# ScalarE's copy of the second group's transposes moved behind four exponentials in an attention kernel

## The chip, the core and the metric

The kernel runs on one NeuronCore of a Trainium2 chip. The metric is the device time of one execution in microseconds (us). The engines are TensorE (PE, with PEld for its weight loads), VectorE (DVE), ScalarE (ACT), GpSimd (POOL) and SyncE (SP), which only issues transfers here.

## What is computed

The input is 64 x 128 rows ("b h") of 128 positions by 64 channels, in float32. Each row is an attention of its own over its 128 positions, behind a batch norm with given mean and variance:

```python
xn = (x - moving_mean) * jax.lax.rsqrt(moving_var + BN_EPS) * gamma + beta
q = xn @ Wq + bq
k = xn @ Wk + bk
v = xn @ Wv + bv
scores = jnp.einsum('bhid,bhjd->bhij', q, k) * d ** (-0.5)
attn = jax.nn.softmax(scores, axis=-1)
out = jnp.einsum('bhij,bhjd->bhid', attn, v)
out = out @ Wo + bo
return xn + out
```

## The kernel before

The kernel folds norm and weights once at the start. w_g stands for the product of the query and key weights, w_o for that of the value and output weights. The 8192 rows are worked in 1024 groups of 8 rows, and the program goes through 512 steps of two groups each: in step t, an even group 2t and an odd group 2t+1 ("the second group"). Each engine has its own instruction stream, written out by hand in its function step(r, t, peeled); the loop body holds four steps, with a few peeled steps ahead of it and behind it. The order on an engine is the order of the calls in its step, and the engines wait for each other by semaphores. A group passes through these stages, several steps apart:

- GpSimd weighs x (L277), adds the bias (L288) and, for three groups of four, makes the last sum y (L299). For the fourth, every other step, VectorE scales in place and adds (L455, L466).
- TensorE projects xT with w_g into one half of tg_ps (L682, two projections a step). ScalarE copies each into g (L360, keep_g).
- TensorE makes the scores of a group in score_ps from g and xT (L624). VectorE finds the row maxima (L490 in two halves for the even group, L480 for the odd) and from them the shift neg_top (L501, L511).
- ScalarE makes the exponentials, 8 a group, one for each row, each with the read of its sum (L335, two instructions each in the profile). The first of an even group waits for neg_top_a_found, the fifth for neg_top_b_found.
- TensorE transposes the 8 probability matrices into tg_ps (L670). For an even group ScalarE copies one half into probsT (L349) and VectorE the other (L549). For an odd group ScalarE copies all of it (L351, keep_probsT).
- TensorE multiplies probabilities and x (L643), VectorE copies the result to uT (L521), TensorE applies w_o (L692), and VectorE scales by the inverted sums into attn (L446).

tg_ps is one buffer of two banks, used in turn by the transposes of the even group, the transposes of the odd group and the two projections. TensorE's projections of step t therefore wait for probsT_a_kept of group 2t-1, which the copy L351 of the same step signals, and the output pair that stands last in the step waits for it and for both copies of g. The odd scores wait for probs_found of the odd group of the step before, since they overwrite its scores.

Of the kernel before, what the change touches and what calls it, by code (L numbers as in the profile page):

```python
# [17 lines left out]
def build(nc: bass.Bass, x, gamma, beta, mean, var, wq, bq, wk, bk, wv, bv, wo, bo, out):  # L18
# [12 lines left out]
    with ExitStack() as ctx:  # L31
# [121 lines left out]
        def uses(r, n):  # L153
            return count(r, n, SEMS, 1)
# [13 lines left out]
        def parts(n):  # L168
            return n % SEMS
# [7 lines left out]
        def pipeline(eng, step):  # L177
            for t in range(-4, BODY):
                step(0, t, True)
            with eng.Fori(2, N // BODY - 1) as r:  # L180
                turn = Turn(eng, r)
                for t in range(BODY // 2):
                    step(turn, t, False)
            for t in range(BODY // 2 + 4):
                step(N // BODY - 1, t, True)
# [5 lines left out]
        def exists(r, n, peeled):  # L191
            return not peeled or 0 <= group(r, n) < N
# [119 lines left out]
        @block.scalar  # L312
        def _(act):
            for i, v in enumerate((gamma, beta, mean, var)):
                act.dma_start(norm_col[:, i:i + 1], v.rearrange("(c o) -> c o", o=1)).then_inc(params_loaded, DMA_INC)
                act.dma_start(norm_row[:, i, :], v.rearrange("(o c) -> o c", o=1).broadcast_to([128, C])).then_inc(params_loaded, DMA_INC)
            act.wait_ge(dve_setup, ROW_VAR)
            nc.scalar.activation(col_tmp[:, 1:2], col_tmp[:, 0:1], ACT.Sqrt).then_inc(act_setup, 1)
            nc.scalar.activation(row_tmp[:, 1, :], row_tmp[:, 0, :], ACT.Sqrt).then_inc(act_setup, 1)

            nc.scalar.activation(exp_first[:], norm_col[:, 3:4], ACT.Exp, scale=-1.0)

            def exponentials(r, n, peeled, rows):
                if not exists(r, n, peeled):
                    return
                s = parts(n)
                if 0 in rows:
                    act.wait_ge((neg_top_a_found if n % 2 == 0 else neg_top_found)[s], uses(r, n))
                    if exists(r, n - 4, peeled):
                        act.wait_ge(probsT_made[s], uses(r, n - 4))  # L330
                        act.wait_ge(sum_inverted[parts(n | 1)], uses(r, (n - 4) | 1))
                for q in rows:
                    if q == HALF and n % 2 == 0:
                        act.wait_ge(neg_top_b_found[s], uses(r, n))
                    last = nc.scalar.activation(probs[:, n % 4, q, :], score_ps[n % 2][:, q // PAIRS, q % PAIRS * W:(q % PAIRS + 1) * W],  # L335
                                                ACT.Exp, bias=neg_top[:, s, q:q + 1], accum_out=prob_sum[:, s, q:q + 1])
                    if q == GROUP - 1:
                        last.then_inc(probs_found[s], 1)

            def keep_probsT(r, n, peeled):  # L340

                if not exists(r, n, peeled):
                    return
                s = parts(n)
                act.wait_ge(probsT_made[s], uses(r, n))
                if exists(r, n - 4, peeled):
                    act.wait_ge(u_made[s], uses(r, n - 4))
                if n % 2 == 0:
                    nc.scalar.activation(probsT_parts[n % 4][:, :, 0], probsT_halves[:, :, 0], ACT.Copy).then_inc(probsT_a_kept[s], 1)  # L349
                else:  # L350
                    nc.scalar.activation(probsT_parts[n % 4], probsT_halves, ACT.Copy).then_inc(probsT_a_kept[s], 1)  # L351

            def keep_g(r, n, peeled):
                if not exists(r, n, peeled):
                    return
                s = parts(n)
                act.wait_ge(g_made[s], uses(r, n))
                if exists(r, n - 4, peeled):
                    act.wait_ge(scores_made[s], uses(r, n - 4))
                nc.scalar.activation(g[:, s].rearrange("p k w -> p (k w)"), tg_ps[:, n % 2],  # L360
                                     ACT.Identity, bias=g_bias[:, 0:1]).then_inc(g_kept[s], 1)

            def step(r, t, peeled):
                keep_probsT(r, 2 * t - 2, peeled)
                exponentials(r, 2 * t, peeled, range(0, 2))
                keep_probsT(r, 2 * t - 1, peeled)
                exponentials(r, 2 * t, peeled, range(2, 8))
                keep_g(r, 2 * t + 2, peeled)
                keep_g(r, 2 * t + 3, peeled)
                exponentials(r, 2 * t + 1, peeled, range(0, 8))  # L370

            pipeline(act, step)

        @block.vector
# [358 lines left out]
```

## Time and profile before

| | us |
|---|---|
| median of 3 runs | 4721.29 (4721.06 to 4724.11) |
| the profiled execution | 4727.12 |
| its span, first to last instruction | 4724.9 |
| PE busy | 4540.1 (96%) |
| DVE busy | 4495.3 (95%) |
| POOL busy | 4508.7 (95%) |
| ACT busy | 4297.6 (91%) |

The granted clock of TensorE is 0.998 of full speed over the span. Busy time is the time with an instruction on the engine; the page further names the chain of work that ended last, the costliest groups of instructions by line with the idle time ahead of them, and the releaser of that idle time. A timeline row gives the start in us from the start of the span, the duration, the engine, the line, the operation and its output and inputs, and in brackets the idle time ahead of it and the engine and line that ended it. Matmul ends are modelled. A row with x4 or x16 is a run of such instructions.

### The profile page before, as it was taken

The page shows a single profiled execution, that of the slowest core. Times are in us where ns is not written, and L with a number is a line of the kernel's source. Part 1 is how long each engine was busy: PE and PEld are TensorE (multiplying, and loading weights), DVE is VectorE, ACT ScalarE, POOL GpSimd, SP SyncE. Part 2 cuts the span into 40 slices and gives each one's busy share as a digit, 9 for nine tenths or more (in the row PEclk, how much of TensorE's full clock was granted, in tenths as well). Part 3 has the DMA queues.
Part 4 walks back from the last instruction along what each step waited for, and adds up shares of the span by engine and source line. Part 5 has one row for each costly group of instructions (what it writes and reads, how often), then busy time and mean ns, then how long its engine had stood idle before and what let it go on. Part 6 is the DMA issues. An engine that isn't in the chain of part 4 may idle for free.

```text
span 4724.9 us, 187136 instructions
## 1 busy us (share of the span) xinstructions
PE 4540.1 (96%) x59416; PEld 3778.9 (80%) x59416; DVE 4495.3 (95%) x7970; ACT 4297.6 (91%) x18437; POOL 4508.7 (95%) x2824
## 2 busy tenths in 40 slices
PE   7999999999999999999999999999999999999999
PEld 5888888888888888888888888888888888888887
DVE  7999999999999999999999999999999999999998
ACT  7999999999999999999999999999999999999998
POOL 7999999999999999999999999999999999999998
PEclk9999999999999999999999999999999999999999
DMA  7888888888888888888888888888888888888886
GB/s 141 174 173 172 173 172 172 172 173 172 173 171 172 172 172 172 172 173 173 171 173 173 172 173 171 172 172 172 172 172 172 173 171 172 173 172 173 171 173 139
DMA packets 4294236, 806.28 MB, mean 171 GB/s; under 512 B 4294208, under 2 KB 4294208, under 8 KB 4294208
## 3 DMA queue, kind: packets, MB, share of 16 engines
q1 hardware_dynamic: 4293312, 805.80, 85.3%
q8 instruction: 15, 0.25, 0.0%
q10 hardware_dynamic: 896, 0.13, 0.0%
q14 instruction: 13, 0.11, 0.0%
HBM read 537.10 MB, written 268.44 MB: 170 GB/s over the span
## 4 chain that ended last, share of the span: by engine, by line
ACT 36%; DVE 26%; PE 20%; issue 15%; DVEq 2%; POOL 1%; DMA 0%; ACTq 0%; POOLq 0%
ACT probs L335 29%; PE uo_ps L643 10%; DVE xT L559 7%; PE score_ps L624 6%; ACT probsT L351 5%; DVE row_stat L530 5%; DVE uo_ps L455 4%; DVE probsT L549 3%; DVE row_stat L490 3%; ACT g L360 3%; PE tg_ps L670 3%; DVE attn L446 2%; DVE neg_top L501 1%; DVE inv_sum L473 1%; PE tg_ps L682 1%
## 5 line engine op out<-in xcount | busy, mean ns | idle before, releaser
L335 ACT ACTIVATE probs<-score_ps,neg_top 128x128 f32<-128x128 f32 x8192 | 2890.5, 384 | 301.9 <-DVE neg_top L501 301.9
L277 POOL TENSOR_TENSOR x_weighted<-x_in,row_weights 128x1024 f32<-128x1024 f32 x1024 | 2402.7, 2371 | 21.8 <-DVE x_weighted L433 21.8
L335 ACT ACTIVATION_READ_ACCUMULATOR probs<-score_ps,neg_top 128x1 f32 x8192 | 1835.5, 224 | 0.0
L624 PE MATMUL score_ps<-xT,g 64*128 64x128 f32 x16384 | 1165.3, 281 | 152.3 <-ACT probs L335 152.3
L624 PEld LDWEIGHTS score_ps<-xT,g 64*128 64x128 f32 x16384 | 1015.1, 188 | 236.9 <-issue 235.4
L288 POOL TENSOR_TENSOR x_scaled_rows<-x_weighted,out_bias 128x512 f32<-128x512 f32 x1024 | 1199.9, 1199 | 0.0
L692 PEld LDWEIGHTS uo_ps<-w_o,uT 128*128 128x128 f32 x8192 | 994.9, 192 | 244.0 <-issue 243.7
L299 POOL TENSOR_TENSOR y<-attn,x_scaled_rows 128x512 f32<-128x512 f32 x768 | 982.3, 1279 | 190.8 <-DVE attn L446 190.8
L682 PE MATMUL tg_ps<-xT,w_g 128*128 128x512 f32 x2048 | 1019.2, 620 | 4.7 <-DVE xT L559 3.5
L643 PE MATMUL uo_ps<-probsT,x_in 128*64 128x128 f32 x16384 | 1008.5, 276 | 0.0
L692 PE MATMUL uo_ps<-w_o,uT 128*128 128x128 f32 x8192 | 997.4, 275 | 0.0
L643 PEld LDWEIGHTS uo_ps<-probsT,x_in 128*64 128x64 f32 x16384 | 884.9, 137 | 34.7 <-issue 0.2
L521 DVE COPY uT<-uo_ps 128x512 f32<-128x512 f32 x1024 | 687.8, 687 | 91.4 <-PE uo_ps L643 74.3
L360 ACT ACTIVATE g<-tg_ps,g_bias 128x512 f32<-128x512 f32 x1024 | 706.6, 711 | 45.8 <-PE tg_ps L682 16.9
L670 PE MATMUL tg_ps<-ident,probs 64*128 64x64 f32 x16384 | 719.3, 226 | 5.3 <-ACT g L360 3.2
L490 DVE TENSOR_REDUCE row_stat<-score_ps 128x4 f32<-128x512 f32 x1024 | 699.3, 683 | 17.5 <-PE score_ps L624 0.9
L670 PEld LDWEIGHTS tg_ps<-ident,probs 64*128 64x128 f32 x16384 | 634.4, 139 | 69.2 <-issue 5.6
L559 DVE STREAM_TRANSPOSE xT<-x_quads 128x1024 f32<-128x1024 f32 x512 | 631.5, 1234 | 0.0
L480 DVE TENSOR_REDUCE row_stat<-score_ps 128x8 f32<-128x1024 f32 x512 | 622.6, 1216 | 1.7 <-PE score_ps L624 1.7
L682 PEld LDWEIGHTS tg_ps<-xT,w_g 128*128 128x128 f32 x2048 | 347.8, 189 | 338.3 <-issue 337.7
L530 DVE TENSOR_REDUCE row_stat<-x_weighted 128x16 f32<-128x1040 f32 x512 | 611.2, 1194 | 2.1 <-POOL x_weighted L277 2.1
L351 ACT ACTIVATE probsT<-tg_ps 128x1024 f32<-128x1024 f32 x512 | 524.1, 1024 | 57.3 <-PE tg_ps L670 57.3
(70 smaller groups left out, 2019.1 us busy)
## 6 DMA issues: line engine op xcount, KB each, us to landing
x_quads<-in_x SPq DMA_DIRECT2D x4096, 64.0 KB, 2.2
x_in<-in_x SPq DMA_DIRECT2D x1024, 256.0 KB, 3.2
out<-y SPq DMA_DIRECT2D x1024, 256.0 KB, 2.4
norm_row<-in_L_conv_gamma ACTq DMA_DIRECT2D x1, 32.0 KB, 2.1
norm_row<-in_L_conv_beta ACTq DMA_DIRECT2D x1, 32.0 KB, 3.7
norm_row<-in_L_conv_bo SPq DMA_DIRECT2D x1, 32.0 KB, 3.4
norm_row<-in_L_conv_moving_mean ACTq DMA_DIRECT2D x1, 32.0 KB, 3.3
norm_row<-in_L_conv_moving_var ACTq DMA_DIRECT2D x1, 32.0 KB, 4.6
```

The lines of the kernel that those rows point to most:

```text
L277: nc.gpsimd.tensor_tensor(x_weighted[:, n % 4, :, 0:2 * C].rearrange("p s (h c) -> p s h c", h=2), x_in[:, n % 8, :, None, :].broadcast_to ...
L288: nc.gpsimd.tensor_tensor(x_scaled_rows[:, n % 8], x_weighted[:, n % 4, :, 0:C], bias_b, ALU.add).then_inc(x_scaled[s], 1)
L299: nc.gpsimd.tensor_tensor(y[:, s], attn[:, s], x_scaled_rows[:, n % 8], ALU.add).then_inc(y_found[s], 1)
L335: last = nc.scalar.activation(probs[:, n % 4, q, :], score_ps[n % 2][:, q // PAIRS, q % PAIRS * W:(q % PAIRS + 1) * W], ACT.Exp, bias=neg_ ...
L360: nc.scalar.activation(g[:, s].rearrange("p k w -> p (k w)"), tg_ps[:, n % 2], ACT.Identity, bias=g_bias[:, 0:1]).then_inc(g_kept[s], 1)
L530: nc.vector.tensor_reduce(row_stat[:, s - 1:s + 1, :, ROW_CONST], x_weighted[:, s - 1:s + 1, :, C:2 * C + 1], AX_X, ALU.add).then_inc(cons ...
L559: nc.vector.transpose(xT[:, n % 8 - 1:n % 8 + 1].rearrange("p g k w -> p (g k w)"), x_quads[:, n % 8 - 1:n % 8 + 1].rearrange("p g k w -> ...
L624: last = nc.tensor.matmul(score_ps[n % 2][:, h, k * W:(k + 1) * W], g[half, s, k, :], xT[half, n % 8, k, :], start=True, stop=True)
L643: last = nc.tensor.matmul(uo_ps[n % 2][h * C:(h + 1) * C, k * W:(k + 1) * W], x_in[:, n % 8, PAIRS * h + k, :], probsT[:, n % 4, PAIRS * h ...
L670: last = nc.tensor.transpose(tg_ps[:, h, q * C:(q + 1) * C], probs[half, n % 4, q, :], ident[half, half])
L682: nc.tensor.matmul(tg_ps[:, n % 2], w_g_all, xT[:, n % 8].rearrange("p k w -> p (k w)"), start=True, stop=True).then_inc(g_made[s], 1)
L692: last = nc.tensor.matmul(o_pairs[n % 2][:, :, k, :], uT[:, n % 2, k, :], w_o_all, start=True, stop=True)
```

## The change

In ScalarE's step, the exponentials of the even group were cut by the copy L351 after the second of eight; now they are cut after the fourth.

```diff
             def step(r, t, peeled):
                 keep_probsT(r, 2 * t - 2, peeled)
-                exponentials(r, 2 * t, peeled, range(0, 2))
+                exponentials(r, 2 * t, peeled, range(0, 4))
                 keep_probsT(r, 2 * t - 1, peeled)
-                exponentials(r, 2 * t, peeled, range(2, 8))
+                exponentials(r, 2 * t, peeled, range(4, 8))
                 keep_g(r, 2 * t + 2, peeled)
```

ScalarE's stream in the loop body before, with the semaphores that each instruction waits for. This is one step (L349 belongs to the even group of the step before, L351 to the odd one of it), up to the exponentials of the odd group:

```order
L349 ACTIVATE probsT<-tg_ps 128x8x64 [waits u_made2,probsT_made2]
L335 ACTIVATE probs,prob_sum<-score_ps,neg_top 128x128 [waits sum_inverted1,probsT_made0,neg_top_a_found0]
L335 ACTIVATE probs,prob_sum<-score_ps,neg_top 128x128
L351 ACTIVATE probsT<-tg_ps 128x1024 [waits u_made3,probsT_made3]
L335 ACTIVATE probs,prob_sum<-score_ps,neg_top 128x128 x2
L335 ACTIVATE probs,prob_sum<-score_ps,neg_top 128x128 [waits neg_top_b_found0]
L335 ACTIVATE probs,prob_sum<-score_ps,neg_top 128x128 x3
L360 ACTIVATE g<-tg_ps,g_bias 128x512 [waits scores_made2,g_made2]
L360 ACTIVATE g<-tg_ps,g_bias 128x512 [waits scores_made3,g_made3]
L335 ACTIVATE probs,prob_sum<-score_ps,neg_top 128x128 [waits sum_inverted1,probsT_made1,neg_top_found1]
```

The same place in the changed kernel:

```order
L335 ACTIVATE probs,prob_sum<-score_ps,neg_top 128x128 [waits sum_inverted1,probsT_made0,neg_top_a_found0]
L335 ACTIVATE probs,prob_sum<-score_ps,neg_top 128x128 x3
L351 ACTIVATE probsT<-tg_ps 128x1024 [waits u_made3,probsT_made3]
L335 ACTIVATE probs,prob_sum<-score_ps,neg_top 128x128 [waits neg_top_b_found0]
L335 ACTIVATE probs,prob_sum<-score_ps,neg_top 128x128 x3
L360 ACTIVATE g<-tg_ps,g_bias 128x512 [waits scores_made2,g_made2]
L360 ACTIVATE g<-tg_ps,g_bias 128x512 [waits scores_made3,g_made3]
```

The first exponential is the one that waits for neg_top_a_found0. The copy L351 has moved behind the third and the fourth exponential, and the one that waits for neg_top_b_found0 now follows it directly.

TensorE's stream has not changed by the edit. This is the place where it waits for the copies, from the odd scores' last pair (the row that waits for probs_found1 too) to the end of the step:

```order
L624 MATMUL score_ps<-xT,g 128x128 [waits probsT_b_kept0,probsT_a_kept0,probs_found1]
L624 MATMUL score_ps<-xT,g 128x128
L670 MATMUL tg_ps<-ident,probs 128x64 x16
L643 MATMUL uo_ps<-probsT,x_in 64x128 [waits attn_kept0,probsT_b_kept2,probsT_a_kept2]
L643 MATMUL uo_ps<-probsT,x_in 64x128 x7
L643 MATMUL uo_ps<-probsT,x_in 64x128 [waits attn_kept1,probsT_a_kept3]
L643 MATMUL uo_ps<-probsT,x_in 64x128 x7
L682 MATMUL tg_ps<-xT,w_g 128x512 [waits probsT_a_kept1,xT_kept1] x2
L692 MATMUL uo_ps<-w_o,uT 128x2x64 [waits u_kept2]
L692 MATMUL uo_ps<-w_o,uT 128x2x64 x3
L692 MATMUL uo_ps<-w_o,uT 128x2x64 [waits u_kept3]
```

The projections L682 stand behind the copy L351 of their own step (probsT_a_kept1), and L643 behind copies of the step before. The numbers behind the names are places in rings of four; this piece is from another of the body's steps, so that the odd group of the step before is 1 here and 3 above. What stands on ScalarE ahead of L351 is ahead of the projections too.

## Rows read from the trace of the kernel before

**Rows 1.** The page: span, busy time by engine, the chain's engines, two lines.

```profile
span 4724.9 us, 187136 instructions
...
PE 4540.1 (96%) x59416; PEld 3778.9 (80%) x59416; DVE 4495.3 (95%) x7970; ACT 4297.6 (91%) x18437; POOL 4508.7 (95%) x2824
...
ACT 36%; DVE 26%; PE 20%; issue 15%; DVEq 2%; POOL 1%; DMA 0%; ACTq 0%; POOLq 0%
...
L360 ACT ACTIVATE g<-tg_ps,g_bias 128x512 f32<-128x512 f32 x1024 | 706.6, 711 | 45.8 <-PE tg_ps L682 16.9
...
L682 PEld LDWEIGHTS tg_ps<-xT,w_g 128*128 128x128 f32 x2048 | 347.8, 189 | 338.3 <-issue 337.7
```

**Rows 2.** Waits of the whole span: who waited, for whom: us, times, longest.

```profile
POOL y L299 <- DVE attn L446: 190.8, 258, 6.3
PE score_ps L624 <- ACT probs L335: 152.3, 511, 1.1
...
ACT probsT L351 <- PE tg_ps L670: 57.3, 258, 1.9
```

**Rows 3.** Timeline of TensorE over two steps: start us, duration, what, wait ahead.

```profile
2401.82 1.98 PE L682 MATMUL tg_ps<-xT,w_g 128*128 128x512 f32 x4
...
2407.47 1.16 PE L624 MATMUL score_ps<-xT,g 64*128 64x128 f32 x16 [0.29 <-ACT probs L335]
...
2409.06 1.97 PE L643 MATMUL uo_ps<-probsT,x_in 128*64 128x128 f32 x32
2410.96 1.98 PE L682 MATMUL tg_ps<-xT,w_g 128*128 128x512 f32 x4
...
2416.62 1.16 PE L624 MATMUL score_ps<-xT,g 64*128 64x128 f32 x16 [0.31 <-ACT probs L335]
...
2420.11 1.98 PE L682 MATMUL tg_ps<-xT,w_g 128*128 128x512 f32 x4
```

**Rows 4.** Timeline of ScalarE over the same two steps.

```profile
2403.01 1.52 ACT L360 ACTIVATE g<-tg_ps,g_bias 128x512 f32<-128x512 f32 x2
...
2408.71 0.37 ACT L335 ACTIVATE probs<-score_ps,neg_top 128x128 f32<-128x128 f32 x1 [0.89 <-DVE neg_top L501]
...
2409.41 1.02 ACT L351 ACTIVATE probsT<-tg_ps 128x1024 f32<-128x1024 f32 x1
2410.31 0.38 ACT L335 ACTIVATE probs<-score_ps,neg_top 128x128 f32<-128x128 f32 x1
...
2412.37 1.32 ACT L360 ACTIVATE g<-tg_ps,g_bias 128x512 f32<-128x512 f32 x2
2413.56 0.38 ACT L335 ACTIVATE probs<-score_ps,neg_top 128x128 f32<-128x128 f32 x1
...
2416.21 0.27 ACT L335 ACTIVATION_READ_ACCUMULATOR probs<-score_ps,neg_top 128x1 f32 x1
...
2417.29 0.37 ACT L335 ACTIVATE probs<-score_ps,neg_top 128x128 f32<-128x128 f32 x1 [0.32 <-DVE neg_top L501]
...
2418.32 1.02 ACT L351 ACTIVATE probsT<-tg_ps 128x1024 f32<-128x1024 f32 x1 [0.22 <-PE tg_ps L670]
```

**Rows 5.** Timeline of VectorE, from the second uT copy to neg_top.

```profile
2401.94 0.69 DVE L521 COPY uT<-uo_ps 128x512 f32<-128x512 f32 x1 [0.18 <-PE uo_ps L643]
...
2408.51 0.17 DVE L501 TENSOR_REDUCE neg_top<-row_stat 128x4 f32<-128x12 f32 x1
...
2409.31 0.17 DVE L501 TENSOR_REDUCE neg_top<-row_stat 128x4 f32<-128x12 f32 x1
```

**Rows 6.** Timeline of both engines at the very start, around the first copy L351.

```profile
41.15 1.02 ACT L351 ACTIVATE probsT<-tg_ps 128x1024 f32<-128x1024 f32 x1 [1.88 <-PE tg_ps L670]
...
42.31 3.75 PE L682 MATMUL tg_ps<-xT,w_g 128*128 128x512 f32 x4 [1.21 <-ACT probsT L351]
```

**Rows 7.** Timeline of both engines one pair of steps later.

```profile
2427.61 1.02 ACT L351 ACTIVATE probsT<-tg_ps 128x1024 f32<-128x1024 f32 x1
...
2429.24 1.12 PE L682 MATMUL tg_ps<-xT,w_g 128*128 128x512 f32 x2
```

## The prediction, made before the run

> **What bounds the kernel now.** I read the page first, then the waits, then one stretch of two steps engine by engine. The page does not name a bound: four engines are busy 91 to 96% of the span and the chain of work changes hands between ScalarE (36%), VectorE (26%) and TensorE (20%) [rows 1]. So the reader has to find the loop that closes on itself. 512 steps in 4724.9 us would be 9.23 us each with start and end included. TensorE's odd scores (the second group's) begin at 2407.47 and 2416.62, 9.15 us apart; its projections at 2401.82, 2410.96 and 2420.11, 9.14 and 9.15 us apart [rows 3]. That even beat is the first sign of the loop, and ScalarE's and VectorE's own starts are not even: the first exponential of a step begins at 2408.71 and 2417.29, 8.58 us apart [rows 4].
>
> The loop, in the step that begins at 2407.47: TensorE runs odd scores, transposes, probabilities times x, and at 2410.96 the two projections, without a wait between them [rows 3]. The projections last 1.98 us, to 2412.94. ScalarE's second copy of g (L360) waits for the second of them: the pair of copies begins at 2412.37 and lasts 1.32 us, and one copy is 0.711 us [rows 1, 4], so the second begins at 2412.37 + 1.32 - 0.71 = 2412.98, 0.04 us behind the projections. Then come the 8 exponentials of the odd group (2413.56 to 2416.48 with the last sum read), and 0.14 us later, at 2416.62, the next odd scores, for which TensorE had waited 0.31 us [rows 3, 4]. From 2407.47 to 2416.62 nothing in this loop waits for anything outside it. The same holds one step earlier: copies of g at 2403.01 lasting 1.52 us put the second at 2403.82, 0.02 us behind the projections' end at 2403.80.
>
> The steps come in two kinds. In every second one ("late" below, here the one with the first exponential at 2408.71), VectorE has just done the in-place scale and add, and ScalarE waits 0.89 us for neg_top; in the others ("early", here 2417.29) it waits 0.32 us [rows 4]. In the early ones the copy L351 then waits about 0.2 us for TensorE's transposes; in the late ones it waits for nothing. The waits count 258 copies of 512 that waited [rows 2], so 254 are late.
>
> **The change part by part.** Two exponentials of the even group go ahead of L351. No instruction is added or removed on any engine. ScalarE's total work between its neg_top wait and the copies of g is the same; only L351 ends later within it. Who waits for L351? In the order of TensorE's instructions, the projections (they overwrite the buffer that L351 reads), and the last output pair, which comes later still.
>
> One exponential with its sum costs (2409.41 - 2408.71)/2 = 0.35 us from start to start [rows 4]; two are 0.69 us when the pace of 0.344 us over the run of them is taken (2412.37 - 2410.31 for six [rows 4]). *Late step:* L351 begins at 2409.41 and lasts 1.02 us, so it ends at 2410.43. It would end at 2411.12. How long TensorE needs from there to its first projection is shown once, at the very start, where it really waited: copy from 41.15 for 1.02 us, projections at 42.31, so 0.14 us [rows 6]; the step from ScalarE's last read to the odd scores gave 0.14 us too. The projections can begin at 2411.26 instead of 2410.96: 0.30 us late. The next late step has a little more room: copy at 2427.61, projections at 2429.24 [rows 7]. 2427.61 + 1.02 + 0.69 + 0.14 = 2429.46, 0.22 us late. Mean 0.26 us.
>
> *Early step:* exponentials from 2417.29, four instead of two, take the copy to 2417.29 + 0.35 + 3 x 0.344 = 2418.67 instead of 2418.32; the transposes are done by then, so its wait of 0.2 us disappears, and the copy is only 0.35 us later. It ends at 2419.69, the projections could begin at 2419.83, and TensorE reaches them at 2420.11 [rows 3, 4]. Cover left: 0.28 us. Cost nothing. Does the wait saved buy anything? ScalarE would reach the first copy of g 0.2 us earlier, but in this kind of step it already waits about 0.2 us for the second projection (1.52 against 1.32 us for the pair). What is late next is that projection, and it has not moved. Gain nothing.
>
> Is 0.26 us per late step on the loop? The projections are at the one place where the loop has no room: ScalarE's second copy of g starts 0.04 us after them, so it and the 8 exponentials and TensorE's next odd scores move with them. And the late step's neg_top does not follow to make it up or make it worse: it hangs on VectorE's own run from its second uT copy (2401.94, which waits for TensorE's L643 in the step before) to neg_top at 2408.51 [rows 5], a distance of 6.6 us that has the loop's beat at one end and nothing of the late copy in it. So each late step is charged anew.
>
> The other waits that the copy is moved past: the exponentials' wait for the second half of neg_top (made from 2409.31 for 0.17 us [rows 5]) stays behind the copy as before, which now ends its turn at 2411.0 instead of 2410.3, and the fifth exponential follows it at once; no wait either way. VectorE's copy L549, GpSimd's and SyncE's queues see the same events in the same order. GpSimd waits 190.8 us in all for VectorE's attn [rows 2] and has room for a longer period.
>
> **Sum.** 254 late steps x 0.26 us = 66 us on the profiled execution's 4727.1 us (span 4724.9), or 4793. The median of the runs shown is 4721.3, so 4787.
>
> Bounds of the unknown size: with no latency behind the copy the delay would be 0.30 - 0.14 and 0.22 - 0.14, mean 0.12 us, 30 us in all; but both rows show 0.14, so I keep it to 0.11 to 0.14, which is 58 to 66 us. Above: when TensorE waits, its weight load is no longer under the matmul before. The mean weight load of the projections is 0.19 us [rows 1]. Had all of it to be paid, the sum would be 254 x 0.45 = 114 us. I take none of it, since the row at 42.31 already stands behind a cold load; and half for the range: 254 x 0.35 = 90, about 4811.
>
> **The rivals.** (1) *No change.* TensorE waits 0.29 and 0.31 us before its odd scores in every step (152.3 us in all) [rows 2, 3]. A delay of 0.26 us at the projections is smaller than that, and if the probabilities it waits for were on ScalarE's own pace it would be swallowed: 4721. This speaks against it: ScalarE's second copy of g starts 0.04 us behind the projections, so the probabilities move too. It decides if that 0.04 us is chance and ScalarE could really start no earlier; in the early step the same distance is 0.02 us while ScalarE had 0.2 us to spare, so it is the wait. Chance 9%. The Trainium skill, "Perfetto Trace Analysis", section "Identifying the Most-Contended Engine", has a rule on this side: the engine with the highest occupancy is the bottleneck, to be optimized first. By it VectorE or GpSimd (95%) would set the time, ScalarE at 91% would have room, and the change would give 4721; this case's even beat of TensorE and uneven one of VectorE speak against it.
>
> (2) *Faster.* If ScalarE's own string of work set the pace, the 57.3 us in 258 waits for the transposes [rows 2] would come off: 4721 - 57 = 4664. It decides where ScalarE, arriving 0.2 us earlier at the copies of g, finds both projections done. The rows show it waiting there in just these steps. Chance 4%.
>
> (3) *Slower by more.* The wait also exposes the weight load, or the early steps' cover of 0.28 us is used up and they too pay. All of the load: 4721 + 114 = 4835. If the early steps lost their cover and paid 0.1 us: 4787 + 26 = 4813. Chance 8% for over 4812.
>
> **How the numbers follow.** Forecast 79%: 4787, from 4772 to 4812 with its bounds. No change 9%, faster 4%, larger loss 8%. Leaving out these last three is 21%; the lower end goes to 4770, since a part of case 1 (some of the delay swallowed) lies just below. A measurement of this kernel can tell about 0.2% from no change, 9.4 us: faster 0.04, same 0.08, slower 0.88.
>
> **What would show it.** In the profile after: L351's waits for TensorE's transposes nearly gone (57.3 us before); a new line, the projections L682 waiting for L351, about 254 times, 0.2 to 0.45 us each; projection starts no longer even but about 9.4 and 9.1 us in turn; the exponentials' waits for neg_top in the step after a late one unchanged at 0.3 us; the pair of g copies in the late step about 1.6 us long instead of 1.32, since ScalarE now arrives ahead of the second projection. Wrong if projections begin at L351's end + 0.14 and yet the odd scores keep 9.14 us, or if the early steps wait too.

## The result

| | median us | runs |
|---|---|---|
| before | 4721.29 | 4721.06 to 4724.11 |
| after | 4784.12 | 4783.02 to 4787.53 |

The ratio is 1.0133 with a 95% interval from 1.011 to 1.0156: the changed kernel is slower by 1.3%, 63 us. The prediction was 4787, from 4770 to 4812.

The page of after, its span, the busy times and the chain's engines:

```profile
span 4785.3 us, 187136 instructions
...
PE 4550.5 (95%) x59416; PEld 3778.8 (79%) x59416; DVE 4519.1 (94%) x7970; ACT 4315.8 (90%) x18437; POOL 4508.8 (94%) x2824
...
DVE 42%; issue 27%; POOL 14%; ACT 11%; PE 5%; DVEq 1%; POOLq 1%; DMA 0%; ACTq 0%
```

The span is 60.4 us longer than in [rows 1], and no engine has that much more work (TensorE 10 us, VectorE 24, ScalarE 18, in overlaps and stretched records). The chain now hands VectorE and GpSimd 56%, where it had given ScalarE 36% and TensorE 20%. It does not name the cause, since nothing was moved on these two engines; but VectorE's work up to neg_top has come to stand on the limiting path of the late steps, as the part on the prediction shows. The cause is read from the waits:

```profile
POOL y L299 <- DVE attn L446: 250.5, 258, 6.3
...
ACT g L360 <- PE tg_ps L682: 102.6, 514, 14.9
PE tg_ps L682 <- ACT probsT L351: 53.5, 251, 1.2
```

The last line is new: 251 times the projections waited for the copy L351, 0.21 us on the mean. The line of L351 waiting for the transposes, 57.3 us before [rows 2], is gone but for 2 us of starting up. GpSimd waits 60 us more for attn than in [rows 2], as much as the span has grown, with the same busy time (4508.8 against 4508.7 us); I read this as a consequence of the longer period and not as its cause.

TensorE over two steps of after, a late one and an early one, to be set against [rows 3]:

```profile
2401.02 1.16 PE L624 MATMUL score_ps<-xT,g 64*128 64x128 f32 x16 [0.29 <-ACT probs L335]
...
2402.60 1.97 PE L643 MATMUL uo_ps<-probsT,x_in 128*64 128x128 f32 x32
2404.82 1.96 PE L682 MATMUL tg_ps<-xT,w_g 128*128 128x512 f32 x4 [0.25 <-ACT probsT L351]
...
2410.45 1.16 PE L624 MATMUL score_ps<-xT,g 64*128 64x128 f32 x16 [0.29 <-ACT probs L335]
...
2412.03 1.97 PE L643 MATMUL uo_ps<-probsT,x_in 128*64 128x128 f32 x32
2413.93 1.98 PE L682 MATMUL tg_ps<-xT,w_g 128*128 128x512 f32 x4
...
2419.58 1.16 PE L624 MATMUL score_ps<-xT,g 64*128 64x128 f32 x16 [0.29 <-ACT probs L335]
```

The odd scores are 9.43 us apart over the late step and 9.13 us over the early one; before, both distances were close to 9.14. The projections begin 2.22 us behind the start of L643 in the late step and 1.90 us in the early one. And ScalarE, against [rows 4]:

```profile
2402.26 0.37 ACT L335 ACTIVATE probs<-score_ps,neg_top 128x128 f32<-128x128 f32 x1 [0.90 <-DVE neg_top L501]
...
2403.65 1.03 ACT L351 ACTIVATE probsT<-tg_ps 128x1024 f32<-128x1024 f32 x1
...
2405.96 0.70 ACT L360 ACTIVATE g<-tg_ps,g_bias 128x512 f32<-128x512 f32 x1
2406.82 0.69 ACT L360 ACTIVATE g<-tg_ps,g_bias 128x512 f32<-128x512 f32 x1 [0.16 <-PE tg_ps L682]
```

The copy ends at 2404.68, the projections' matmuls begin 0.14 us later, and the second copy of g begins at 2406.82, 0.04 us behind the projections' end at 2406.78.

### The profile page after: what moved, and what is told of

Same layout as the page of the kernel before. It is cut to its first block, busy times and chain, and to the rows that moved or that the text cites. A ratio compares the mean times of both kernels' runs of the same rounds, so it can differ in the third digit from the quotient of the medians.

```text
span 4785.3 us, 187136 instructions
## 1 busy us (share of the span) xinstructions
PE 4550.5 (95%) x59416; PEld 3778.8 (79%) x59416; DVE 4519.1 (94%) x7970; ACT 4315.8 (90%) x18437; POOL 4508.8 (94%) x2824
## 4 chain that ended last, share of the span: by engine, by line
DVE 42%; issue 27%; POOL 14%; ACT 11%; PE 5%; DVEq 1%; POOLq 1%; DMA 0%; ACTq 0%
POOL x_weighted L277 13%; DVE xT L559 12%; DVE row_stat L530 10%; ACT probs L335 6%; DVE attn L446 6%; ACT probsT L351 5%; PE tg_ps L682 4%; DVE uo_ps L455 4%; DVE probsT L549 3%; DVE row_stat L490 3%; DVE neg_top L501 1%; DVE neg_top L511 1%; DVE inv_sum L473 1%; POOL y L299 1%; DVE y L466 0%
## 5 line engine op out<-in xcount | busy, mean ns | idle before, releaser
L624 PE MATMUL score_ps<-xT,g 64*128 64x128 f32 x16384 | 1165.1, 281 | 149.7 <-ACT probs L335 149.7
L682 PE MATMUL tg_ps<-xT,w_g 128*128 128x512 f32 x2048 | 1011.8, 616 | 57.2 <-ACT probsT L351 53.5
L643 PE MATMUL uo_ps<-probsT,x_in 128*64 128x128 f32 x16384 | 1008.5, 276 | 0.0
L643 PEld LDWEIGHTS uo_ps<-probsT,x_in 128*64 128x64 f32 x16384 | 884.7, 137 | 34.6 <-issue 0.2
L670 PE MATMUL tg_ps<-ident,probs 64*128 64x64 f32 x16384 | 718.8, 225 | 5.0 <-ACT g L360 3.2
L670 PEld LDWEIGHTS tg_ps<-ident,probs 64*128 64x128 f32 x16384 | 633.9, 139 | 68.9 <-issue 5.6
L682 PEld LDWEIGHTS tg_ps<-xT,w_g 128*128 128x128 f32 x2048 | 347.8, 189 | 401.2 <-issue 400.6
L446 DVE TENSOR_TENSOR attn<-uo_ps,inv_sum 128x512 f32<-128x512 f32 x768 | 529.5, 689 | 63.2 <-PE uo_ps L692 52.8
```

Source lines behind the costliest of these rows:

```text
L624: last = nc.tensor.matmul(score_ps[n % 2][:, h, k * W:(k + 1) * W], g[half, s, k, :], xT[half, n % 8, k, :], start=True, stop=True)
L643: last = nc.tensor.matmul(uo_ps[n % 2][h * C:(h + 1) * C, k * W:(k + 1) * W], x_in[:, n % 8, PAIRS * h + k, :], probsT[:, n % 4, PAIRS * h ...
L670: last = nc.tensor.transpose(tg_ps[:, h, q * C:(q + 1) * C], probs[half, n % 4, q, :], ident[half, half])
L682: nc.tensor.matmul(tg_ps[:, n % 2], w_g_all, xT[:, n % 8].rearrange("p k w -> p (k w)"), start=True, stop=True).then_inc(g_made[s], 1)
```

## The experiments

All runs are shown with the median of the runs of before that stood beside them on the same chip.

| run | change against before | us | before beside it | ratio (95%) |
|---|---|---|---|---|
| e1_three | three ahead of L351 | 4721.7 | 4721.7 | 0.9999 (0.9989 to 1.0008) |
| e2_late_only | four, in late steps only | 4781.3 | 4721.7 | 1.0126 (1.011 to 1.0143) |
| e3_early_only | four, in early steps only | 4721.3 | 4721.7 | 0.9998 (0.9988 to 1.0008) |
| e4_six | six | 5049.0 | 4721.7 | 1.0693 (1.0675 to 1.0711) |
| e5_one | one | 4788.4 | 4725.6 | 1.013 (1.0113 to 1.0147) |
| e7_project_first | projections ahead of odd product | 4963.9 | 4725.6 | 1.0505 (1.0487 to 1.0522) |
| e8_project_first_b | the same, VectorE's copy earlier | 5148.9 | 4725.6 | 1.0896 (1.0878 to 1.0914) |
| e9_x_early | even product ahead of odd scores, two | 4747.5 | 4725.1 | 1.0048 (1.0032 to 1.0065) |
| e10_x_early_three | the same, three | 4727.9 | 4725.1 | 1.0006 (0.9996 to 1.0015) |
| e11_x_half_early | half of the even product, three | 4641.0 | 4725.1 | 0.9821 (0.9805 to 0.9838) |
| e12_half_by_step | the same, two late, three early | 4614.3 | 4724.9 | 0.9765 (0.9749 to 0.9782) |
| e13_half_four | the same as e11, four | 4729.0 | 4724.9 | 1.0009 (0.9999 to 1.0019) |

### Three ahead instead of four

```diff
-                exponentials(r, 2 * t, peeled, range(0, 2))
+                exponentials(r, 2 * t, peeled, range(0, 3))
                 keep_probsT(r, 2 * t - 1, peeled)
-                exponentials(r, 2 * t, peeled, range(2, 8))
+                exponentials(r, 2 * t, peeled, range(3, 8))
```

> The copy L351 stands behind three exponentials of the even group instead of two (before) or four. Theory (the projections wait for the end of L351 plus about 0.11 us, and only what goes past their old start costs): late step copy ends at 2410.43 + 0.34 = 2410.77 on the time of before, plus 0.11 is 2410.88, 0.07 us ahead of the weight load at 2410.95; no cost, 4721 us, and no wait of L682 for L351. Rival (each exponential moved ahead costs the same, whatever waits for the copy): half of the 63 us, 4753 us.

Measured: 4721.7 us, no change. The wait of L682 for L351 is not there but for the one of starting up (1.2 us, 1 time). A cost for each exponential moved would have shown as 32 us against an interval of about 5. There is a threshold, and it lies between three and four.

### Four ahead in one kind of step

```diff
+                ahead = 4 if t % 2 == 0 else 2
-                exponentials(r, 2 * t, peeled, range(0, 2))
+                exponentials(r, 2 * t, peeled, range(0, ahead))
                 keep_probsT(r, 2 * t - 1, peeled)
-                exponentials(r, 2 * t, peeled, range(2, 8))
+                exponentials(r, 2 * t, peeled, range(ahead, 8))
```

This is the edit for the late steps; for the early ones 4 and 2 are exchanged.

> Four exponentials ahead of L351 only in the steps with even t (the late ones, where the first exponential waits 0.9 us for neg_top), two in the others. Theory (the whole loss is made in the late steps): 4784 us, about 250 waits of L682 for L351. Rival (both kinds of steps pay by what is moved): half of the loss, 4753 us.

> Four exponentials ahead of L351 only in the steps with odd t (the early ones, where the first exponential waits 0.3 us and the copy waited 0.2 us for the transposes), two in the others. Theory: no cost and no gain, 4721 us, although the waits of L351 for the transposes (57 us) go away. Rival (ScalarE's string sets the time in these steps): 57 us faster, 4664. Rival (both kinds pay): 4753.

Measured: 4781.3 us with the late steps changed, 4721.3 us with the early ones. So 59.5 of the 63 us are made in the late steps and none in the early ones. Waits of the late-only kernel (a line is added, so L682 is L683 and L670 is L671):

```profile
PE tg_ps L683 <- ACT probsT L351: 53.2, 251, 1.2
...
ACT probsT L351 <- PE tg_ps L671: 50.3, 257, 0.8
```

The projections wait as in after, and the early steps' waits of L351 have stayed. In the early-only kernel both lines are down to starting up (1.2 and 1.5 us), and the time is that of before: the 57 us of waits for the transposes were taken away and nothing was gained. ScalarE waits for the projections at the copies of g instead, 81.2 us where it had been 16.9. The rest of 3 us between after (4784.1) and late-only (4781.3) is about what the runs of each spread over.

### Six ahead

The same edit as the first, with range(0, 6) and range(6, 8).

> Six exponentials ahead of L351 in all steps. Theory: in the late step the delay grows by two more exponentials, 0.25 + 0.69 = 0.94 us; in the early step the room of 0.26 us (copy end 2419.69 plus 0.11 against 2420.11 is 0.3) is used up and 0.69 - 0.30 = 0.39 us is paid; together 1.33 us for two steps, 254 x 1.33 = 338 us, 5059 us. Rival (each exponential moved costs the same, 31 us): 4721 + 4 x 31 = 4847 us. Rival (only late steps ever pay): 4721 + 254 x 0.94 = 4960 us.

Measured: 5049.0 us, 327 us over before, where the loop gave 338 and the two rivals 126 and 239. Projections of two steps and the waits of the span:

```profile
2406.19 1.97 PE L643 MATMUL uo_ps<-probsT,x_in 128*64 128x128 f32 x32
2408.56 1.96 PE L682 MATMUL tg_ps<-xT,w_g 128*128 128x512 f32 x4 [0.40 <-ACT probsT L351]
...
2415.76 1.97 PE L643 MATMUL uo_ps<-probsT,x_in 128*64 128x128 f32 x32
2418.59 1.96 PE L682 MATMUL tg_ps<-xT,w_g 128*128 128x512 f32 x4 [0.86 <-ACT probsT L351]
```

```profile
PE tg_ps L682 <- ACT probsT L351: 310.7, 509, 2.2
```

Now both kinds of step wait, the early one 0.40 us, the late one 0.86. From the start of L643 the early projections come after 2.37 us instead of 1.90, so they are 0.47 us late. Two exponentials more than with four are 0.69 us; the early steps' cover is real, and with four ahead about 0.22 us of it was left, where the prediction had 0.28.

### One ahead

The same edit with range(0, 1) and range(1, 8).

> The copy L351 stands behind one exponential of the even group instead of two. The projections gain nothing by an earlier copy (they are reached by TensorE at 2410.96 and 2420.11, later than the copy's end plus 0.11). In the late step the copy would wait to 2409.17 for the transposes instead of starting at 2409.06, so ScalarE reaches the copies of g 0.1 us later; it had 0 to 0.1 us to spare there. In the early step the copy starts at 2418.32 as before but one exponential more stands behind it: 0.34 us later at the copies of g, where ScalarE had waited 0.2. Theory: 0.05 + 0.14 us for two steps, about 48 us, 4770 us. Rival (the copy's place costs only when it is late): 4721 us.

Measured: 4788.4 us against 4725.6, 63 us slower, where 48 were expected and the rival had said none. The direction held, the sum did not. ScalarE's copies L351 over three steps, and between the first two the copies of g:

```profile
2402.14 1.02 ACT L351 ACTIVATE probsT<-tg_ps 128x1024 f32<-128x1024 f32 x1
...
2405.47 1.31 ACT L360 ACTIVATE g<-tg_ps,g_bias 128x512 f32<-128x512 f32 x2
2406.61 0.42 ACT L335 ACTIVATE probs<-score_ps,neg_top 128x128 f32<-128x128 f32 x1
...
2411.40 1.03 ACT L351 ACTIVATE probsT<-tg_ps 128x1024 f32<-128x1024 f32 x1 [0.67 <-PE tg_ps L670]
...
2420.66 1.02 ACT L351 ACTIVATE probsT<-tg_ps 128x1024 f32<-128x1024 f32 x1 [0.21 <-PE tg_ps L670]
```

The copies L351 are 9.26 us apart in both kinds of step. With the copy so early another loop has closed: copy, seven exponentials, both copies of g back to back (1.31 us), eight exponentials, odd scores, transposes, and the copy again, which always starts with the transposes' end. 9.26 - 9.14 = 0.12 us, in all 512 steps: 61 us. I had charged the late steps only 0.05 us, by the room that ScalarE had at its copies of g in before; but once every copy hangs on the transposes, both kinds pay the same. So the place of the copy is bounded on both sides: of the five tried (one, two, three, four, six) two and three are the good ones.

### Shortening the loop: the projections first

If the loop runs through the projections, moving work from ahead of them to behind them should shorten it. TensorE's and VectorE's steps:

```diff
-                probs_times_x(r, 2 * t - 3, peeled)
                 project(r, 2 * t + 2, peeled)
                 project(r, 2 * t + 3, peeled)
+                probs_times_x(r, 2 * t - 3, peeled)
...
-                keep_u(r, 2 * t - 3, peeled)
                 find_shift(r, 2 * t + 1, peeled)
                 transpose_x(r, 2 * t + 7, peeled)
                 find_const(r, 2 * t + 3, peeled)
+                keep_u(r, 2 * t - 3, peeled)
```

> An attempt at a faster kernel by shortening the loop: TensorE makes both projections ahead of the odd group's product of probabilities and x, and VectorE's copy of that product (uT of group 2t-3) stands behind find_const; ScalarE as before. Theory: in the early step the projections could start at the copy's end plus 0.11, 0.66 us earlier, but ScalarE itself reaches its second copy of g only 0.2 us earlier than now; in the late step ScalarE is no earlier at all, since neg_top sets it. So 0.2 us for two steps, 4670 us, if VectorE keeps its times. Rival: VectorE's uT copy comes about 2 us later and TensorE's last output waits for it by about 0.4 us a step, which goes to the even scores and neg_top: no gain or slower, 4721 to 4900 us.

> The same, with VectorE's copy of the odd group's product ahead of find_const: it would wait about 0.5 us for TensorE each step but release TensorE's last output earlier. Theory and rival as in the run beside it: 4670 us if VectorE has the room (it is busy 17.5 of 18.3 us for two steps), else slower by up to 0.3 us a step, 4870 us.

Measured: 4963.9 and 5148.9 us, the rivals' side. The waits of the first:

```profile
ACT probs L335 <- DVE neg_top L501: 686.4, 511, 1.6
...
PE tg_ps L682 <- ACT probsT L351: 295.0, 510, 1.2
DVE attn L446 <- PE uo_ps L692: 164.9, 512, 0.5
DVE uo_ps L455 <- PE uo_ps L692: 116.8, 256, 0.6
```

The waits for neg_top have more than doubled from the 302 us of before, on which this run is built. The odd product comes later, VectorE's uT copy later, TensorE's outputs with it, and VectorE waits for these (282 us) ahead of the work that ends in neg_top. In the second, VectorE waits 599 us for the product itself. I read this so: the old loop was shortened, and a longer one through VectorE took its place. This does not show that the theory of the loop is right; the next runs do.

### Shortening the loop from the other side

The even group's product is ready long before, and TensorE waits 0.29 us ahead of the odd scores. It can stand there, ahead of the loop, and nothing of VectorE is made late by it.

```diff
                 scores(r, 2 * t, peeled, range(PAIRS))
+                probs_times_x(r, 2 * t - 4, peeled)
                 scores(r, 2 * t + 1, peeled, range(PAIRS - 1))
...
-                probs_times_x(r, 2 * t - 4, peeled)
                 probs_times_x(r, 2 * t - 3, peeled)
```

> The other way into the same loop. TensorE makes the even group's product of probabilities and x (16 matmuls, 0.95 us, ready long before) between the even and the odd scores, where it waited 0.3 us a step, instead of ahead of the odd group's product. ScalarE as before, two exponentials ahead of L351. If the loop is odd scores, transposes, products, projections, second g copy, 8 exponentials, it gets 0.95 us shorter, and what is next is TensorE's own work, 9.14 - 0.3 = 8.84 us a step, or ScalarE's loop through the transposes (seen with one exponential ahead at 9.26 us, so 9.26 - 0.34 = 8.92 with two): 8.92 x 512 = 110 us less, about 4612 us. Rival: TensorE now reaches the odd scores 0.65 us after their probabilities are done, which delays transposes and copy as much, and ScalarE's loop through them grows: 9.14 us or more, 4721 us or slower.

> The same with three exponentials ahead of L351. If ScalarE's loop through the transposes is what is next, this takes 0.34 us more off it, and TensorE's own 8.84 us or VectorE's (busy 8.8 us a step) is left: 4721 - 512 x 0.3 = 4567 us. If the copy then holds up the projections instead (they come 0.95 us earlier behind the odd scores), slower than the run beside it.

Measured: 4747.5 us with two exponentials ahead of L351, 4727.9 with three. Neither gained, against 4612 and 4567 expected. TensorE in the one with three:

```profile
2408.48 0.66 PE L670 MATMUL tg_ps<-ident,probs 64*128 64x64 f32 x16
2409.08 1.09 PE L643 MATMUL uo_ps<-probsT,x_in 128*64 128x128 f32 x16
2410.35 1.95 PE L682 MATMUL tg_ps<-xT,w_g 128*128 128x512 f32 x4 [0.18 <-ACT probsT L351]
```

Between the end of the odd transposes and the projections there is now only one product, and TensorE waits in every step (510 times, 95.3 us). The copy that the projections wait for is itself 1.03 us long, begins about 0.04 us behind the transposes and needs 0.14 us behind its end: 1.2 us that one product of 0.95 to 1.0 us can't cover. The 0.3 us of waiting was taken from ahead of the odd scores and came back ahead of the projections. With two ahead L351 waits 335.0 us for the transposes, against 133.3 us with three. That this makes the further 20 us is likely, but was not worked out.

### Half of the product

```diff
                 scores(r, 2 * t, peeled, range(PAIRS))
+                probs_times_x(r, 2 * t - 4, peeled, range(2))
                 scores(r, 2 * t + 1, peeled, range(PAIRS - 1))
...
-                probs_times_x(r, 2 * t - 4, peeled)
+                probs_times_x(r, 2 * t - 4, peeled, range(2, PAIRS))
                 probs_times_x(r, 2 * t - 3, peeled)
```

with the product's waits only at its first pair, its signal only at its last, and three exponentials ahead of L351.

> Half of that product (two of four pairs, 0.48 us) moved ahead of the odd scores, three exponentials ahead of L351. The loop gets 0.48 us shorter, TensorE reaches the odd scores 0.18 us late: also bound by 8.84 us of TensorE, 4567 us, if TensorE is what is next; between the two others if it is the lateness of the odd scores.

Measured: 4641.0 us, 84 us faster than before, though 74 us over the 4567 expected for the case that only TensorE's own 8.84 us a step were left. TensorE no longer waits for the probabilities, and one and a half products, 24 matmuls in 1.53 us, cover the copy but for 0.18 us in the late steps:

```profile
2403.59 1.53 PE L644 MATMUL uo_ps<-probsT,x_in 128*64 128x128 f32 x24
2405.23 1.95 PE L684 MATMUL tg_ps<-xT,w_g 128*128 128x512 f32 x4
...
2412.67 1.53 PE L644 MATMUL uo_ps<-probsT,x_in 128*64 128x128 f32 x24
2414.13 1.98 PE L684 MATMUL tg_ps<-xT,w_g 128*128 128x512 f32 x4
```

The first pair is a late step, the second an early one (lines are one or two further down than in before): 1.64 us from start to start in the late step, 1.46 in the early one. That difference is the next run:

```diff
+                ahead = 2 if t % 2 == 0 else 3
-                exponentials(r, 2 * t, peeled, range(0, 3))
+                exponentials(r, 2 * t, peeled, range(0, ahead))
                 keep_probsT(r, 2 * t - 1, peeled)
-                exponentials(r, 2 * t, peeled, range(3, 8))
+                exponentials(r, 2 * t, peeled, range(ahead, 8))
```

> The kernel with half of the even product ahead of the odd scores, and the copy L351 behind two exponentials in the late steps and three in the early ones (instead of three in all). There TensorE waits 0.18 us for L351 in every second step, although it no longer waits for the probabilities. Theory: TensorE's own work now sets the time, so this wait counts in full: 255 x 0.18 = 46 us less, 4595 us. Rival: VectorE, which shows no wait of over 0.15 us in a stretch of two steps, sets it: 4641 us, no change.

Measured: 4614.3 us, 27 less than with three everywhere (46 expected) and 2.35% less than before. It is the fastest version here. The stretch from 1000 to 4000 us (busy us of each engine with the number of instructions), first of this kernel, then of before:

```profile
1000.00:4000.00 3000.00, 3000.00 (x38995) 2460.76 (x38996) 2924.88 (x5210) 2813.74 (x12101) 2960.05 (x1850) 1.00 0.89 176
```

```profile
1000.00:4000.00 3000.00, 2902.85 (x38096) 2417.87 (x38098) 2876.04 (x5092) 2752.49 (x11815) 2890.36 (x1806) 1.00 0.86 172
```

TensorE has no gap left in 3000 us; GpSimd is close behind it, busy 98.7% of the stretch. Its timeline of one step (lines of this kernel stand one to three further down than in before):

```profile
2402.04 1.11 PE L625 MATMUL score_ps<-xT,g 64*128 64x128 f32 x16
2403.08 0.66 PE L645 MATMUL uo_ps<-probsT,x_in 128*64 128x128 f32 x8
2403.66 1.16 PE L625 MATMUL score_ps<-xT,g 64*128 64x128 f32 x16
...
2405.25 1.53 PE L645 MATMUL uo_ps<-probsT,x_in 128*64 128x128 f32 x24
2406.71 1.99 PE L685 MATMUL tg_ps<-xT,w_g 128*128 128x512 f32 x4
...
2412.59 1.16 PE L625 MATMUL score_ps<-xT,g 64*128 64x128 f32 x16
```

The odd scores are 8.93 us apart. That is TensorE's own work in a step of this kernel, where I had put it at 8.84 (9.14 less 0.3 of waiting). Two things went wrong in that figure. The split costs: the products take 0.58 and 1.46 us to the next start, 2.04 together, against 1.90 in one piece [rows 3], 0.14 us more. And the wait that was filled was worth more than its bracket: from the start of the even scores to the start of what follows them it is 1.40 us in before (2406.07 to 2407.47) and 1.04 us here (2402.04 to 2403.08), 0.36 us less and not 0.3. The bracket begins at the modelled end of the even scores (2406.07 + 1.11), and here the next matmuls start 0.07 us ahead of such an end. 0.14 - 0.06 us makes 0.08 of the 0.09. Why this run won 27 us and not 46 can be read off the kernel with three everywhere: the 0.18 us is that of one late step, the next one has 2421.59 to 2423.14, 1.55 us, 0.09 over the early ones. The mean of 0.135, less the 0.03 that a stretch begun after a wait gives back (below), is 0.105 us, and times 255 it is 27.

Last, the change of this case on the half-product kernel: four ahead in all steps.

```diff
-                exponentials(r, 2 * t, peeled, range(0, 3))
+                exponentials(r, 2 * t, peeled, range(0, 4))
                 keep_probsT(r, 2 * t - 1, peeled)
-                exponentials(r, 2 * t, peeled, range(3, 8))
+                exponentials(r, 2 * t, peeled, range(4, 8))
```

> The same kernel with four exponentials ahead of L351 in all steps, that is the change of this case made on it. In the late steps the copy ends 0.34 us later and the projections with it. If TensorE's own work or the loop through the projections has no room: 255 x 0.34 = 87 us more than with three, 4728 us, or more if early steps pay too. If VectorE sets the time and TensorE has room behind it: 4641 us.

Measured: 4729.0 us, 88 us over the one with three, against 87 expected: a late step pays the whole 0.34 us of one exponential, because its room was used up already. Its late projections show it:

```profile
2415.22 1.96 PE L684 MATMUL tg_ps<-xT,w_g 128*128 128x512 f32 x4 [0.46 <-ACT probsT L351]
```

## Why the prediction was right, point by point

**The loop.** Odd scores, transposes, products, projections, second copy of g, eight exponentials: it was found by the even beat of TensorE, although the page named no bound. That the projections are the place on it that the copy reaches is shown by runs of three kinds: nothing happens until the projections are reached late (three ahead), every further 0.34 us is paid once they are (six ahead, and four ahead on the half-product kernel), and work moved out of the loop makes the kernel faster until something else closes (half of the product).

**The late step.** Predicted 0.30 and 0.22 us in turn, mean 0.26. The waits read 0.25 us at 2404.82 and 0.17 us in the next late step, but these brackets begin at the modelled end of the matmuls before. By the distance of the projections from the start of L643 the first late step is 2.22 - 1.90 = 0.32 us late, and by the odd scores it is 9.43 - 9.14 = 0.29 us long. The next late step has its projections 2.13 us behind L643 and ends with the odd scores at 2428.92:

```profile
2421.17 1.97 PE L643 MATMUL uo_ps<-probsT,x_in 128*64 128x128 f32 x32
2423.30 1.96 PE L682 MATMUL tg_ps<-xT,w_g 128*128 128x512 f32 x4 [0.17 <-ACT probsT L351]
...
2428.92 1.16 PE L624 MATMUL score_ps<-xT,g 64*128 64x128 f32 x16 [0.29 <-ACT probs L335]
```

These are 9.34 us behind those at 2419.58, so it is 0.20 us long. The mean is 0.245, and over the span 60.4 / 254 gives 0.24 us, where I had 0.26. Two small misses lie in this: at the projections the delay is 0.32 and 0.23 us, 0.01 to 0.02 more than predicted, and behind them 0.03 us is given back, which the sum did not have. The 0.14 us behind the copy is right for the matmul, but the weight load begins 0.11 us behind the copy, and the projections then take 0.02 to 0.03 us less until their work is handed on (1.96 against 1.98 us). The one miss makes the sum 0.015 us a late step too small and the other 0.03 us too large; that they partly cancel is luck. The half of a weight load that stood in the range was not needed.

**The early step.** Predicted nothing lost (0.28 us of cover) and nothing gained by the 57 us of waits taken away. The early-only run shows both, 4721.3 us; with six ahead the early step starts to pay as it should.

**VectorE does not follow.** The distance from the second uT copy to neg_top was 2401.94 to 2408.51, 6.57 us [rows 5]. In after the timeline of VectorE has

```profile
2395.49 0.69 DVE L521 COPY uT<-uo_ps 128x512 f32<-128x512 f32 x1 [0.18 <-PE uo_ps L643]
...
2402.06 0.17 DVE L501 TENSOR_REDUCE neg_top<-row_stat 128x4 f32<-128x12 f32 x1
...
2414.05 0.69 DVE L521 COPY uT<-uo_ps 128x512 f32<-128x512 f32 x1 [0.18 <-PE uo_ps L643]
```

again 6.57 us. So each late step is charged anew, and the waits for neg_top are as they were, 0.90 and 0.34 us.

The rows show one thing more, which the prediction used and did not name: the limiting loop of after is another than that of before. In the late step of after the projections wait for the copy, the copy for four exponentials, these for neg_top, and neg_top comes from VectorE's run behind the uT copy at 2395.49. What TensorE does meanwhile (odd scores, transposes, products) is done 0.32 us before the projections can start and no longer decides. Only in the early step does the path run through it, down to the products at 2412.03 and the next such uT copy at 2414.05. That is a loop of two steps, 18.56 us = 9.43 + 9.13, with VectorE's 6.57 us in it. In before it was nearly as long: from the first copy of g to the exponentials ScalarE took 1.19 us in the late step [rows 4], and where it never waits for the projections it takes 1.14 us (2405.47 to 2406.61 with one exponential ahead), so there ScalarE, coming from neg_top, was 0.05 us earlier than the projections let it be (0.14 us in the late step before that one, 2394.02 to 2395.30). No run here shortened VectorE's part; that this would speed up after is read from the rows only.

**The signs named ahead.** They came: L351's waits gone, L682's waits in their place (251 for 254, of 0.25 and 0.17 us in turn, the second just below the 0.2 named), unequal steps (9.43 and 9.13 for about 9.4 and 9.1), the pair of g copies 1.55 us long instead of 1.32 (about 1.6 was said).

**The rivals.** "Swallowed by TensorE's 0.3 us wait" fell with the result: that wait is still there, 149.7 us, since the probabilities moved with the projections. The rule of the Trainium skill's "Perfetto Trace Analysis", section "Identifying the Most-Contended Engine", to go by occupancy, was weighed with it. This case's measurement decides against reading room from it: ScalarE, at 91% the least busy of the four engines, had one copy moved by 0.69 us, and that cost 63 us. It does not follow that the busier engines were off the path; VectorE's work is on it in the late steps of after. "Faster" fell with the early-only run. "Slower by more" did not occur with four ahead and did with six.

## What to carry to other kernels

When four engines are all busy above 90%, look for the loop. In this kernel the event that came at even distances was on it, and a start 0.02 to 0.04 us behind another engine's end marked where it passes on. Look also for a second loop that is nearly as long: here a change of 0.69 us to the place of one copy made it the longer one. Then ask of a moved instruction not how busy its engine is, but who waits for it and how late that one gets there; the answer is a threshold (here an estimated 0.07 us of room with three exponentials and a measured mean loss of 0.24 us with four), and alternating steps have thresholds of their own, which can be served one by one. To gain, move work out of the loop into the wait that it leaves, and check that what remains still covers the transfer or copy that hid beneath it: the whole product gained nothing, half of it 1.8%.

## What the runs showed of the hardware that was not expected

One copy moved by 0.69 us turned the chain that ended last from ScalarE and TensorE (56% together) to VectorE and GpSimd (56%). Two paths had stood within 0.05 to 0.14 us of each other in the late steps of before, and the shares of the chain do not show how close a second path is.

A run of exponentials starts every 0.34 us, whatever the records' durations, which grow from 0.36 to 0.43 us along a run; the mean of 384 ns and the separate 224 ns of the sum's read would give 0.61. The starts are the price, not the durations.
